# Gate statistics of batches 2 and 3 taken from token rows in the delta rule's opening, filter pieces there through four banks, corner products interleaved

## The reference, cut to what matters

```python
q, k, v = silu(conv4(x @ q_w.T)), silu(conv4(x @ k_w.T)), silu(conv4(x @ v_w.T))
beta = sigmoid(x @ b_w.T)
# delta rule by chunks: inv = inverse of a unit lower triangular matrix, u = inv @ v, w = inv @ kb,
# and a recurrence over the chunks that carries a state S and gives delta_out
short, long_, wide = fir(v, fir_s), fir(v, fir_l), fir(v, fir_wd)      # 3, 31 and 64 taps
gate_in = concat([x, stats(short), stats(long_), stats(wide), stats(delta_out), stats(v)])
# stats(t): per token and head mean(t), sqrt(mean(t*t)), max|t|
# a two layer gate then mixes short, long_, wide, delta_out and v
```

## Time and profile before

| | before |
|---|---|
| median of 3 runs | 689.45 us (686.68 to 690.70) |
| profiled execution | 692.56 us, its span 690.8 us |
| PE busy | 585.1 us (85%), granted clock 0.944 of full |
| DVE, ACT, POOL busy | 455.0 us (66%), 283.7 us (41%), 117.2 us (17%) |
| instructions | 16962 |

### The profile page before, as it was taken

The page is one execution under the profiler, slowest core; times in us unless marked ns, Lnnn a source line. Parts: engine busy times, 40 slices in busy tenths (PEclk is TensorE's granted clock), DMA queues, the critical chain, the costliest instruction groups (busy, mean ns, idle before and its releaser), DMA issues. The chain is left out here.

```text
span 690.8 us, 16962 instructions
## 1 busy us (share of the span) xinstructions
PE 585.1 (85%) x7436; PEld 426.7 (62%) x7448; DVE 455.0 (66%) x890; ACT 283.7 (41%) x518; POOL 117.2 (17%) x102
## 2 busy tenths in 40 slices
PE   5878779999999999898996767699999758988984
PEld 2555567777768677776543436588787644555642
DVE  2976327767785786764858899464466754676664
ACT  1867324433443344333354542333324054544531
POOL 1001340160042006010011223362000010000000
PEclk9989989999999999998999987899999888999988
DMA  6600520140051004122510107100000000000001
GB/s 176 213 1 1 186 92 3 66 151 5 3 154 64 4 16 141 34 94 59 186 40 24 31 30 233 32 1 1 0 1 1 0 0 1 1 30 1 31 10 52
DMA packets 26538, 37.51 MB, mean 54 GB/s; under 512 B 4642, under 2 KB 13603, under 8 KB 26464
## 3 DMA queue, kind: packets, MB, share of 16 engines
q1 hardware_dynamic: 26463, 36.42, 16.5%
HBM read 34.31 MB, written 2.10 MB: 53 GB/s over the span
## 5 line engine op out<-in xcount | busy, mean ns | idle before, releaser
L298 DVE SCALAR_TENSOR_TENSOR arena<-bank,conv_w,arena 128x511 f32<-128x511 f32 (+2 forms) x72 | 53.2, 746 | 20.0 <-ACT arena L461 13.6
L1508 POOL COPY arena<-v_win 128x256 f32<-128x256 f32 x32 | 19.8, 644 | 178.5 <-PE bank L787 178.5
L1960 ACT COPY arena<-bank 128x512 f32<-128x512 f32 x40 | 23.3, 586 | 55.4 <-PE bank L1763 35.9
L1763 PE MATMUL bank<-v_win,arena 128*128 128x256 f32 x192 | 45.2, 384 | 0.0
L787 PE MATMUL bank<-arena 128*32 128x128 f32 x512 | 35.7, 409 | 9.3 <-ACT arena L1147 7.7
L2535 PE MATMUL bank<-v_win,arena 128*128 128x256 bf16 x288 | 36.5, 279 | 8.0 <-DVE arena L2622 7.0
L1197 ACT COPY arena<-bank 128x512 f32<-128x512 f32 x40 | 21.7, 590 | 48.3 <-PE bank L909 48.3
L1763 PEld LDWEIGHTS bank<-v_win,arena 128*128 128x128 f32 x192 | 36.8, 193 | 5.3 <-issue 0.4
L2525 PE MATMUL bank<-arena,v_win 128*128 128x512 bf16 x134 | 36.2, 400 | 3.7 <-DVE arena L2593 3.2
L1152 ACT COPY arena<-bank 128x256 f32<-128x256 f32 x32 | 19.3, 604 | 48.2 <-PE bank L800 48.1
L2535 PEld LDWEIGHTS bank<-v_win,arena 128*128 128x128 bf16 x288 | 28.4, 100 | 16.7 <-DVE arena L2622 8.0
(11 more groups left out here) (279 smaller groups left out, 1368.5 us busy)
## 6 DMA issues: line engine op xcount, KB each, us to landing
arena<-in_toep_w SPq DMA_DIRECT2D x32, 256.0 KB, 3.0
arena<-in_toep_l SPq DMA_DIRECT2D x32, 256.0 KB, 3.8
arena<-in_xT SPq DMA_DIRECT2D x12, 512.0 KB, 4.2
arena<-in_x SPq DMA_DIRECT2D x4, 512.0 KB, 3.9
arena<-in_ctx SPq DMA_DIRECT2D x4, 512.0 KB, 4.4
out<-arena SPq DMA_DIRECT2D x4, 512.0 KB, 2.9
qkv_w<-in_qkv_wT SPq DMA_DIRECT2D x1, 768.0 KB, 5.5
v_win<-in_w_gateT SPq DMA_DIRECT2D x1, 768.0 KB, 4.8
```

The costliest lines, as they stand in the source:

```text
L298: return nc.vector.scalar_tensor_tensor(out=acc[:, j:L], in0=src[:, 0:L - j], scalar=conv_w[:, m, CONV_K - 1 - j:CONV_K - j], in1=acc[:, j:L],
L1508: g.tensor_copy(A2["v_piece"][:, n % 2, :, :].rearrange("p c (t two) -> p t two c", two=2), v_win[:, :, :, n * PIECE:(n + 1) * PIECE].rear ...
L1763: i = mm(oo, src[:, k, f * P:(f + 1) * P], w[:, k, :], start=(k == 0), stop=(k == KT - 1 and f > 0))
L1960: nc.scalar.copy(dst(i), bank[RING_FIRST + n % RING].rearrange("p (t c) -> p t c", c=dst(i).shape[-1]))\
```

## The change: what it does

1. **First block.** `head_sums`, `turn_sums`, the squares, `rows_out` and `sums_out` of batches 2 and 3 are gone from PE's and ACT's lists. Both lists are reordered: `silus(3)` directly behind `silus(2)`; `project_keys(0)` and `(1)` ahead of `turn_v(3)`; `project_keys(2)` behind it; the key taps and the key silus on ACT follow.
2. **Opening.** Sum and sum of squares of `short` and v of batches 2 and 3 are taken from token rows: four ACT squares of 1024 values per partition (`square_rows`, into `delta`, which is not yet written then) and eight DVE sums (`row_sum`, `row_squares`). `output_out(b, 0)` waits for the last of them. ACT's `gate_constants` (a load of the table for Exp and two tiny operations) moves from ahead of `q_squares` to the end of the opening.
3. **Opening, banks.** The windows of pieces 0 to 7 alternate between banks 4 and 5, the token results between 2 and 3. `filter_piece(n)` no longer waits for the last piece's windows nor for `fir_out`, but for the windows of piece n - 2; `to_tokens(n)` waits for its windows, for `fir_out` of piece n - 2 and, for n = 0, for `beta_th`.
4. **`blocks_back`, all four batches.** The products L941 are interleaved with those of L932, one behind each pair, and both semaphore increments come at the end.

```diff
@@ PE, first block
                 turn_sums(1)
+                project_keys(0)
+                project_keys(1)
                 turn_v(3)
-                project_keys(0)
+                project_keys(2)
                 turn_short(2)
-                project_keys(1)
-                project_keys(2)
-                head_sums(2)
-                turn_sums(2)
                 turn_short(3)
                 project_keys(3)
-                head_sums(3)
-                turn_sums(3)
@@ ACT, first block
                 silus(2)
+                silus(3)
                 v_out(2)
                 rows_out(1)
-                silus(3)
+                key_tap_last(0)
                 sums_out(1)
+                key_tap_last(1)
                 v_out(3)
-                v_squares(2)
-                key_tap_last(0)
-                short_squares(2)
-                key_tap_last(1)
+                key_tap_last(2)
                 short_out(2)
-                v_squares(3)
-                key_tap_last(2)
-                rows_out(2)
-                short_squares(3)
-                sums_out(2)
                 key_silu(0)
                 short_out(3)
                 key_tap_last(3)
                 key_silu(1)
-                rows_out(3)
                 key_silu(2)
-                sums_out(3)
                 key_silu(3)
@@ banks and the pieces' waits on PE
-        fir_bank = lambda n: bank[5 if n < OPENING else 3]
+        fir_bank = lambda n: bank[4 + n % 2 if n < OPENING else 3]
+        tok_bank = lambda n: bank[2 + n % 2 if n < OPENING else 3]
+        FROM_ROWS = [(SHORT, 2), (PLAIN, 2), (SHORT, 3), (PLAIN, 3)]
...
-                    if n:
+                    if n >= OPENING:
                         pe.wait_ge(s2["windows_out"].sem, n)
-                    behind = n if first else n - 1
-                    if behind > 0:
-                        pe.wait_ge(s2["fir_out"].sem, behind)
+                        pe.wait_ge(s2["fir_out"].sem, n if first else n - 1)
+                    elif n >= 2:
+                        pe.wait_ge(s2["windows_out"].sem, n - 1)
...
                     pe.wait_ge(s2["windows_out"].sem, n + 1)
+                    if n == 0:
+                        pe.wait_ge(s2["beta_th"].sem, 1)
+                    elif 2 <= n < OPENING:
+                        pe.wait_ge(s2["fir_out"].sem, n - 1)
@@ blocks_back
                     for t2 in range(2):
                         for e in range(2):
                             for p in range(KT):
                                 c, t = (4 * t2 + 2 * e + p) * DK, 2 * th + t2
-                                i = mm(turn_bank(th)[DK:P, c:c + DK], A2["cross"][0:DK, t, e, p, :],
+                                for a in range(2):
+                                    i = mm(zw_bank(th, a)[half(a), c:c + DK], A2["X"][half(a), t, e, p, :],
+                                           ident_half(a), start=True, stop=True)
+                                j = mm(turn_bank(th)[DK:P, c:c + DK], A2["cross"][0:DK, t, e, p, :],
                                        A2["X"][0:DK, t, e, p, :], start=True, stop=True)
                     i.then_inc(s2["end_mm"].sem, 1)
+                    j.then_inc(s2["end_mm"].sem, 1)
@@ ACT, opening
+                def square_rows(j):
+                    n, k = FROM_ROWS[j]
+                    a(rows_squared(j), branch(n, k), ACT.Square).then_inc(s2["rows_sq"].sem, 1)
...
                 beta_tanh(0)
-                gate_constants()
                 q_squares(0)
                 filter_out(0, first=True)
                 filter_out(1)
                 filter_out(2)
+                square_rows(0)
                 filter_out(3)
                 k_back_out(0, 0, 1)
                 filter_out(4)
+                square_rows(1)
+                filter_out(5)
                 cross_out(0, 0)
-                filter_out(5)
+                filter_out(6)
                 cross_out(0, 1)
-                filter_out(6)
+                square_rows(2)
                 filter_out(7)
                 tokens_out(OPENING - 1)
+                square_rows(3)
+                gate_constants()
@@ DVE, opening
+                def row_sum(j):
+                    n, k = FROM_ROWS[j]
+                    v.tensor_reduce(stat_of(k, n, 0), branch(n, k), AX.X, ALU.add)
+
+                def row_squares(j):
+                    n, k = FROM_ROWS[j]
+                    dve.wait_ge(s2["rows_sq"].sem, j + 1)
+                    v.tensor_reduce(stat_of(k, n, 1), rows_squared(j), AX.X, ALU.add).then_inc(s2["rows_red"].sem, 1)
...
                 q_sums(0)
+                row_sum(0)
                 k_scale(0, 0)
                 k_scale(0, 1)
+                row_sum(1)
+                row_squares(0)
+                row_sum(2)
                 gram_masks(0, 0)
                 gram_masks(0, 1)
+                row_squares(1)
+                row_sum(3)
+                row_squares(2)
+                row_squares(3)
```

More of the change, by code:

```diff
@@ L269, in layer @@
             "x_turned": 10, "xt_out": 12, "end_mm": 6, "full_out": 6, "ks_mm": 3, "r_out": 3,
-            "u_mm": 4, "u_out": 4, "s_mm": 3, "s_out": 3, "o_mm": 4, "o_out": 4, "squared": 0, "job_red": 0, "corner": 0,
+            "u_mm": 4, "u_out": 4, "s_mm": 3, "s_out": 3, "o_mm": 4, "o_out": 4, "squared": 0, "job_red": 0, "rows_sq": 0, "rows_red": 0, "corner": 0,
             "v_copied": 1, "fir_mm": 1, "windows_out": 1, "turn_mm": 1, "fir_out": 1}, ())
@@ L469, in v_squares @@
                 def v_squares(b):
-                    if b >= 2:
-                        act.wait_ge(s1["sums"].sem, s1["sums"].at(b - 2, 1))
                     for m in range(KT):
@@ L496, in rows_out @@
                     act.wait_ge(s1["sums"].sem, s1["sums"].at(b, 1))
-                    if b >= 2:
-                        act.wait_ge(s1["rows_turned"].sem, s1["rows_turned"].at(b - 2, 1))
                     nc.scalar.copy(A1[b % 2]["rows"], sums_bank[:, 0:P]).then_inc(s1["rows_out"].sem, 1)
@@ L694, in squares_of, with rows_squared @@
             return x.rearrange("p (t h c) -> p t h c", t=TT, h=H) if JOBS[j][0] == DELTA else x.rearrange("p (t c) -> p t c", c=DK)
+        def rows_squared(j):
+            return delta[:, j * TT:(j + 1) * TT, :].rearrange("p t (h c) -> p t h c", h=H)
         def evens(ap, k):
@@ L799, in to_tokens @@
                                 col = D + f * P + c4 * DK
-                                i = mm(fir_bank(n)[half(par), col:col + DK], A2["fir_s"][:, 2 * c4 + f, :],
+                                i = mm(tok_bank(n)[half(par), col:col + DK], A2["fir_s"][:, 2 * c4 + f, :],
                                        const["select"][:, half(par)], start=True, stop=True)
@@ L926, in blocks_back @@
                     pe.wait_ge(s2["x_out"].sem, s2["x_out"].at(b, 20 + 2 * th + 2))
-                    for t2 in range(2):
-                        for e in range(2):
-                            for p in range(KT):
-                                for a in range(2):
-                                    c = (4 * t2 + 2 * e + p) * DK
-                                    i = mm(zw_bank(th, a)[half(a), c:c + DK], A2["X"][half(a), 2 * th + t2, e, p, :],
-                                           ident_half(a), start=True, stop=True)
-                    i.then_inc(s2["end_mm"].sem, 1)
                     if th == 0:
@@ L1152, in tokens_out @@
                     nc.scalar.copy(filtered[:, :, :, n * PIECE:(n + 1) * PIECE].rearrange("p f t c -> p f c t"),
-                                   fir_bank(n)[:, D:2 * D].rearrange("p (f c t) -> p f c t", f=2, c=PIECE))\
+                                   tok_bank(n)[:, D:2 * D].rearrange("p (f c t) -> p f c t", f=2, c=PIECE))\
                         .then_inc(s2["fir_out"].sem, 1)
@@ L1432, in output_out @@
                         dve.wait_ge(s2["norms"].sem, s2["norms"].at(b, 2))
+                        dve.wait_ge(s2["rows_red"].sem, len(FROM_ROWS))
                         if b == B - 1:
```

## The result

The changed kernel takes 683.87 us in the median of 4 runs (679.61 to 685.06) against 689.63 us: ratio 0.990, interval 0.9868 to 0.9931. It is 5.8 us faster by the medians (4.8 to 9.1 by the interval) where 8.2 were forecast. The profiled execution took 685.06 us, 7.5 us less than that of before.

A forecast was written before the change was run, and what follows sets the result against it. No engine is full in the first block's second half or the opening; waits between engines bound both. First block 2.6, opening 4.1, `blocks_back` 2.7, less 1.2 for the clock: 8.2 us, median 681.3 us, range 677.0 to 686.2.

The forecast's parts named there:

- Opening: Opening's filter pieces, a ping-pong in one bank: minus 4.1 us, bounds 2.5 to 5.1; `attend` at 90.0 instead of 94.11.
- Piece 3: Opening: piece 3 starts with POOL's copy behind `k_root`, at 74.4 instead of 77.31, 2.9 us earlier.
- the pieces' period: Sign in the opening: time from one filter piece to the next under 2.1 us, against 2.84 before.
- Corners: `blocks_back`, products side by side in three array quarters, limited by DVE's copies: 0.67 us per batch, minus 2.7 us, bounds 0 to 3.6.
- First block: First block, DVE's list ends it: minus 2.6 us, bounds 1.3 to 3.4; last key silu ends at 62.1 instead of 64.88.
- Table load: Opening: `gate_constants` moved out of the way of `q_squares`, 1.5 us, among the reasons pieces 0 to 2 finish earlier.
- The clock: PE's 4.05 us rest at the barrier puts `beta` and `turn_k` at 1.2 GHz: plus 1.2 us, bounds 0 to 2.0.
- A: Rival: low clock turns it round, needing 18 us more at 1.2 GHz between 62 and 105 us; 694 with 28; chance 0.03.
- B: Rival: opening gives half, 1.5 to 2.0 us instead of 4.1, as another chain ends it; 683.7 us; chance 0.15.
- C: Rival: within 0.5%; B, first block 1.3 us at the low clock, corner products 1 us; 686.1 us; chance 0.12.
- E: Rival: the three array quarters don't overlap in `blocks_back`, so the corners give nothing; 684.0 us; chance 0.06.
- D: Rival: low-clock stretch at the start of `inverse(0)` goes too, some 2 us more won; 679.3 us; chance 0.15.

The follow-up runs named there:

- the two traces: The changed kernel profiled first and then run again with no edit: medians 683.87 us and 684.15 us.
- both additions: Changed kernel plus 12 added products at the end of the first block and 4 and 3 around the opening's last token turn: 679.69 us, ratio 0.9823.
- the pair at full clock: Changed kernel with 12 added products at the end of the first block, with old corner order against new: 681.51 us against 678.22 us.
- the first experiments: Changed kernel again, 684.15 us; with old corner order, 684.52; with one bank for the opening's pieces, 681.90; with first block of before and no row statistics, 682.53.

## Why the prediction was right or wrong

*Opening: right in its steps.* `attend` was to come 24.9 us after `beta`, plus up to 1.2 for the clock: 25.47 and 25.2 in the two traces, 23.7 with the clock up, which is 1.2 less than forecast at like clock. Piece 3 was bound by POOL's copy, the third square cost 0.5 us, the last sum was covered by 0.2 us (0.1 forecast), and with the clock up it is uncovered: with both additions the masks start at 87.05, 1.7 us behind the attention product's start, and 1.2 us behind it where the sums come later (88.16 and 86.96). I allowed 0.9 us for waits that I couldn't count, and these were less. One sign failed in part: the pieces' period was to be under 2.1 us, and from piece 5 to piece 6 it is 2.2 in the first trace.

*Corners: right.* 0.76 us a batch, 0.67 forecast: `corner(0, 1)` waited for DVE's fourth copy as argued, which ended 4.04 us after the first identity product, while the products of `blocks_back` took 2.09 us instead of 3.42. The forecast counted four batches alike. Three give 2.3 us; the last gave 0.6 in the first pair of traces and nothing in the pair at full clock, where all four together make 2.5 us (2.7 forecast).

*First block: right on the mean.* 2.6 forecast, with bounds of 1.3 to 3.4; the last key silu ended 2.0 and 3.8 us earlier in the two traces, with more and less of the low clock in them, so the second lies outside the bounds.

*Table load:* I had it among the reasons of the opening's gain. With the clock up in both, the opening is as long with the load in front (23.66 us) as at the end (23.74), so it has no part in it.

*The clock: the term that was too small.* The sign was right, and so was the one place that it priced: the rest at the barrier is 4.04 us (4.05 forecast), `beta` starts at 1.2 GHz, and the opening is 1.5 to 1.8 us longer than with the rest filled (1.2 forecast, 2.0 at most). But the time lost more than that. The whole execution's mean clock fell from 0.951 (45 executions of the kernel before, 0.943 to 0.957) to 0.943 (the ten of the changed one, 0.939 to 0.947). A straight line through those 45 falls by 5.5 us for 0.01 of clock, with 1.3 us of scatter about it. 0.008 is thus 4.4 us where I had 1.2. This is an estimate: it carries a line of one kernel over to another. The line at 0.950 gives 690.6 us, the changed kernel moved to 0.950 along it 679.9: 10.7 us of shortening at like clock, where my terms without the clock made 9.4. So the gain of the edits was somewhat under- and the clock's share more clearly underestimated, and the time came out at 683.9 instead of 681.3. That it lies well inside the range is in part luck, since the two errors offset each other.

Why the mean of the whole fell stays open. The rest at the barrier alone doesn't do it: the kernel with the old corners (mean 0.9505) and the one with one bank (0.9513) have the same rest of 4.04 and 4.05 us and the clock of the kernel before. No trace of an execution of before at its usual 0.951 was taken, so where the 11 us more at 1.2 GHz lie isn't shown either.

The same line settles what the first experiments left open. Moved along it to a clock of 0.950, the means are 679.9 us for the changed kernel, 684.8 with the old corners, 682.5 with one bank and 683.1 with the first block of before, each good to about 0.6. So each part is worth something at like clock, 4.9, 2.6 and 3.2 us, though in the plain times all three had looked like nothing. With the products added at the end of the first block it is 681.2: by this line their whole gain is the clock's.

Something of this I could have seen beforehand: a profile is one execution. That of before had a clock of 0.944, near the lowest of its kernel, so that the pair of profiles, at 0.944 and 0.942, differs by 7.5 us and the medians by 5.8. In first block, opening, loop and the rest, the trace of before has 6.8, 3.4, 10.2 and 57.3 us at 1.2 GHz, that of after 8.8, 5.0, 6.7 and 58.9: 77.7 and 79.4 in sum, so that this pair didn't show what the medians paid.

Over all traces the count is this. With the rest at the barrier the clock was low at `beta` or fell within 1.2 us behind it in 5 of 5 (the changed kernel twice, old corners, one bank, products in the opening only); with work in its place, `head_sums` or added products, it was up in 9 of 9. At the start of `inverse(0)` it was up in 4 of 4 with the products in the opening; without them it was low, or fell within 1 us, in 6 and up in 4; chance alone would give a split this clear in 7 of 100 cases, so here the cause is likely and not shown.

*The rivals.* A (the clock turns it round) was right in kind and too high in amount: some 11 us more at 1.2 GHz (0.008 x 2 x 684) instead of the 18 that it takes, and the traces don't place them between 62 and 105 us, where A had put them. B and C did not happen in the trace, E neither (C also took 2.2 us for the opening where B has 1.5 to 2.0). D did not happen in the changed kernel's two traces; it did with products added in the opening, and in four of the seven other traces of kernels that hold the change in whole or in part.

*The better version* is the changed kernel with 12 products that compute nothing at the end of the first block: 0.9818 (0.9769 to 0.9867) of the kernel before, 678.2 us. With those in the opening instead it is 678.7, within what can be told apart.

## What to carry to other kernels

When work is taken off TensorE where it waits anyway, look at what it does just after the gap that opens: here 4 us of rest before a barrier cost 1.5 to 1.8 us of the opening, and products that compute nothing, put into that rest, brought them back. Judge a part of under 1% by its own stretch of the trace and by runs of like clock; the whole time alone said of the corners and the banks that they were worth nothing, and at full clock their stretches are worth 2.5 and 3.8 us. And of two orders on an engine, ask what the next engine's list waits for: of 1.3 us that TensorE gained in `blocks_back` VectorE's copies let 0.76 through.

## What the runs showed of the hardware

The low clock has a price that can be read: across 45 executions of one kernel 0.01 less of the mean clock goes with 5.5 us more, which is an estimated 0.4 us for each microsecond at 1.2 GHz (0.01 x 2 x 690 = 13.8 us of it). With no edit at all, the place of the low stretches moved from run to run, and with it the end of the first block by 1.7 us and `inverse(0)` by 1.5. In three quarters of the array products with 64 x 64 weights ran side by side without slowing each other: 218 ns a record as alone, 58 ns from set to set, the three of a set started within 13 ns, and 48 records started in 0.94 us.
